# Mixture-of-experts stage on one Trainium2 core: rounding the expert weights to fp32r on ScalarE instead of GpSimd

## The reference

```
probs = softmax(xt @ Wg);  wts, idx = top_k(probs, 2);  wts = wts / sum(wts)
h1 = gelu(einsum('td,edf->etf', xt, W1) + b1[:, None, :])      # W1: 8 x 256 x 1024
ye = einsum('etf,efd->etd', h1, W2) + b2[:, None, :]           # W2: 8 x 1024 x 256
moe_out = sum(wts[..., None] * ye[idx, arange(T)[:, None], :], axis=1)
x = layernorm(x + (x_attn + moe_out))
```

## Time and profile before

| | |
|---|---|
| median of 3 runs | 4782.31 us (4779.12 to 4784.58) |
| the profiled execution | 4777.63 us, span 4775.8 us |
| busy in the whole span | PE 4253.5 us (89%), DVE 3625.5, ACT 3703.7, POOL 2061.1 |
| experts stage, from the first up to the last down | 4122.2 to 4675.5 us |
| mean granted TensorE clock | 0.942 |

### The profile page before, as it was taken

The page is one execution under the profiler, slowest core; times in us unless marked ns, Lnnn a source line. Parts: engine busy times, 40 slices in busy tenths (PEclk is TensorE's granted clock), DMA queues, the critical chain, the costliest instruction groups (busy, mean ns, idle before and its releaser), DMA issues. The chain is left out here.

```text
span 4775.8 us, 95820 instructions
## 1 busy us (share of the span) xinstructions
PE 4253.5 (89%) x22137; PEld 1697.9 (36%) x22137; DVE 3625.5 (76%) x7256; ACT 3703.7 (78%) x6958; POOL 2061.1 (43%) x1018
## 2 busy tenths in 40 slices
PE   7569999999999999999999999999999963499991
PEld 4322222222222222222222222222222243499991
DVE  3658898989899889988898998889898863133335
ACT  1347999999999999999999999999999841255551
POOL 0011343434344443434343443434343423788875
PEclk8777999999999999999999999999999985699995
DMA  2231010101001010101011010101010014334433
GB/s 78 101 83 17 0 17 0 17 0 17 5 12 17 0 17 0 17 0 17 0 17 16 2 17 0 17 0 17 0 17 0 0 51 140 123 138 137 137 115 114
DMA packets 105461, 176.13 MB, mean 37 GB/s; under 512 B 16512, under 2 KB 87552, under 8 KB 99072
## 3 DMA queue, kind: packets, MB, share of 16 engines
q1 hardware_dynamic: 86864, 146.17, 11.9%
q0 software_dynamic: 6336, 16.79, 1.1%
q10 hardware_dynamic: 12144, 12.06, 0.7%
HBM read 117.55 MB, written 57.15 MB: 37 GB/s over the span
## 5 line engine op out<-in xcount | busy, mean ns | idle before, releaser
L741 ACT ACTIVATE probs<-s_ps 128x512 f32<-128x512 f32 x4096 | 2430.6, 601 | 213.5 <-PE s_ps L683 161.3
L590 POOL TENSOR_TENSOR probs_low<-probs 128x1024 f16<-128x1024 f32 x640 | 1324.6, 2070 | 2082.9 <-ACT probs L741 2082.9
L804 DVE TENSOR_TENSOR probs_low<-probs 128x1024 f16<-128x1024 f32 x1408 | 1820.5, 1295 | 20.9 <-ACT probs L741 20.7
L797 DVE CUSTOM_DVE_ANT_0 excess<-b_ps,excess 128x512 f32<-128x512 f32 x2048 | 1401.9, 687 | 332.5 <-ACT excess L728 264.7
L683 PE MATMUL s_ps<-q_ring,k_ring 98*128 (+1 forms) x4096 | 1565.1, 384 | 13.8 <-ACT probs L741 8.6
L728 ACT ACTIVATE excess<-diff_ps 128x512 f32<-128x512 f32 x2048 | 1215.4, 594 | 57.9 <-PE diff_ps L627 48.9
L666 PE MATMUL o_ps<-probs,v_parts 128*64 128x512 bf16 x4106 | 854.1, 412 | 74.8 <-ACT o_here L733 72.2
L683 PEld LDWEIGHTS s_ps<-q_ring,k_ring 98*128 98x128 bf16 x4096 | 434.3, 106 | 1160.3 <-ACT probs L741 574.1
L627 PE MATMUL diff_ps<-kd_ring,q_ring 96*128 (+1 forms) x2048 | 801.1, 391 | 50.5 <-issue 38.2
L636 PE MATMUL b_ps<-k_ring,q_ring 96*128 (+1 forms) x2048 | 798.9, 390 | 11.5 <-DVE unit_max L797 10.7
L666 PE MATMUL o_ps<-probs_low,v_parts 128*64 128x512 f16 x4106 | 783.7, 378 | 0.0
(11 more groups left out here) (195 smaller groups left out, 3445.3 us busy)
## 6 DMA issues: line engine op xcount, KB each, us to landing
w_in<-in_W SPq DMA_DIRECT2D x46, 1024.0 KB, 4.9
q_ring<-qs_dram SPq DMA_DIRECT2D x96, 128.0 KB, 4.4
k_ring<-ks_dram SPq DMA_DIRECT2D x96, 128.0 KB, 7.1
slots_dram<-zero_rows SPq DMA_DIRECT2D x24, 512.0 KB, 6.4
rows_e<-slots_dram SPq DMA_DIRECT2D x24, 512.0 KB, 3.9
y_slots_dram<-y_out ACTq DMA_DIRECT2D x23, 512.0 KB, 4.1
qs_dram<-parts SPq DMA_DIRECT2D x16, 384.0 KB, 3.0
ks_dram<-parts SPq DMA_DIRECT2D x16, 384.0 KB, 4.2
```

The source lines that it names most:

```text
L590: nc.gpsimd.tensor_tensor(probs_low[:, t % BUFS, :, :], probs[:, t % BUFS, :, :], high[:, :, :, 1], ALU.subtract).then_inc(pool_low_done, 1)
L741: nc.scalar.activation(probs[:, t % BUFS, k, :], s2_ps[:, k, :], ACT.Exp).then_inc(exp_done, 1)
L797: nc.vector.tensor_tensor_reduce(excess[:, u % 2, :], b_ps[:, u % 2, :], excess[:, u % 2, :], 1.0, LEAST, ALU.add, ALU.max, unit_max[:, u ...
L804: nc.vector.tensor_tensor(probs_low[:, t % BUFS, :, :], probs[:, t % BUFS, :, :], high[:, :, :, 1], ALU.subtract).then_inc(low_done, 1)
```

## The change

The high parts of the weights are no longer made by GpSimd but by ScalarE, in four copies a tile of 128x1024 elements each. They stand inside ScalarE's tile j for the weights of tile j+1: the halves of `w1` after the `hidden_high` copies of steps 1 and 2, the halves of `w2` after those of steps 6 and 7. GpSimd keeps the subtractions, each behind a wait for its ScalarE copy; that of `w2` is now done in two halves (so there are four instructions, two for each matrix). `w_ready` counts four a tile, and TensorE waits for all four at the tile's start as before. So that the last tile rounds nothing, `per_tile` takes the last two tiles out of the loop.

```diff
-        W_OPS = 6
+        W_OPS = 4
...
-                body(0, 0, True)
-                with eng.Fori(0, (SLOT_TILES - 1) // 2) as it:
+                body(0, 0, True, False)
+                with eng.Fori(0, (SLOT_TILES - 3) // 2) as it:
                     for n in range(2):
-                        body(eng.snap(it * 2 + (n + 1)), (n + 1) % 2, False)
+                        body(eng.snap(it * 2 + (n + 1)), (n + 1) % 2, False, False)
+                body(SLOT_TILES - 2, 1, False, False)
+                body(SLOT_TILES - 1, 0, False, True)
...
-                pool.wait_ge(ups_done, j + 1)
-                pool.wait_ge(w1_full, j * 16)
                 w1 = w1_in[:, :, :].rearrange("p j (i t) -> p j t i", t=FT)
                 for half in range(HALVES):
-                    nc.gpsimd.tensor_tensor(w1_high[:, b, half, :, :], w1[:, half, :, :],
-                                            zero[:, :].unsqueeze(2).to_broadcast([P, FT, P]), ALU.add
-                                            ).then_inc(w_ready, 1)
-                pool.wait_ge(w_ready, j * W_OPS + 2)
-                for half in range(HALVES):
+                    pool.wait_ge(w1_rounded, j * HALVES + (half + 1 - HALVES))
+                    pool.sem_inc(pool_passed, 1)
                     nc.gpsimd.tensor_tensor(w1_low[:, b, half, :, :], w1[:, half, :, :],
                                             w1_high[:, b, half, :, :].bitcast(F32), ALU.subtract).then_inc(w_ready, 1)
+                pool.wait_ge(w_ready, j * W_OPS + 2)
+                pool.sem_inc(w1_split, 1)
+
+                for half in range(2):
+                    part = slice(FT // 2 * half, FT // 2 * half + FT // 2)
+                    pool.wait_ge(w2_rounded, j * 2 + (half - 1))
+                    pool.sem_inc(pool_passed, 1)
+                    nc.gpsimd.tensor_tensor(w2_low[:, b, part, :], w2_in[:, part, :], w2_high[:, b, part, :].bitcast(F32),
+                                            ALU.subtract).then_inc(w_ready, 1)
                 pool.wait_ge(w_ready, j * W_OPS + 4)
-                pool.sem_inc(w1_split, 1)
-
-                pool.wait_ge(hidden_used, j * FT + (4 - FT))
-                pool.wait_ge(w2_full, j * 16)
-                nc.gpsimd.tensor_tensor(w2_high[:, b, :, :], w2_in[:, :, :],
-                                        zero[:, :].unsqueeze(2).to_broadcast([P, FT, D]), ALU.add).then_inc(w_ready, 1)
...
                 pool.sem_inc(w2_split, 1)
...
-                pe.wait_ge(w_ready, j * W_OPS + 6)
+                pe.wait_ge(w_ready, j * W_OPS + 4)
...
+            def round_w1(j, b, half):
+
+                act.wait_ge(ups_done, j + 1)
+                act.wait_ge(w1_full, j * 16)
+                nc.scalar.activation(w1_high[:, b, half, :, :],
+                                     w1_in[:, half, :].rearrange("p (i t) -> p t i", t=FT), ACT.Copy).then_inc(w1_rounded, 1)
+
+            def round_w2(j, b, half):
+
+                act.wait_ge(hidden_used, j * FT + (4 - FT))
+                act.wait_ge(w2_full, j * 16)
+                part = slice(FT // 2 * half, FT // 2 * half + FT // 2)
+                nc.scalar.activation(w2_high[:, b, part, :], w2_in[:, part, :], ACT.Copy).then_inc(w2_rounded, 1)
...
                     nc.scalar.activation(hidden_high[:, f % 4, :], h_ps[:, f % 2, :], ACT.Copy).then_inc(high_done, 1)
+                    if f in (1, 2) and not last:
+                        round_w1(j + 1, 1 - b, f - 1)
+                    if f in (6, 7) and not last:
+                        round_w2(j + 1, 1 - b, f - 6)
                     if f == 4 and not first:
                         store(j - 1)
```

More of the change, by code:

```diff
@@ L1256, in experts @@
             sem("w1_full"), sem("w2_full"), sem("w1_split"), sem("w2_split"), sem("w_ready"))
+        w1_rounded, w2_rounded = sem("w1_rounded"), sem("w2_rounded")
         sync_passed, pool_passed = sem("sync_passed_e"), sem("pool_passed_e")
@@ L1292, in load_bias, with load @@
                 sp.dma_start(b2_here[:, b, :], dram["b2"][ds(e, 1), :].to_broadcast([P, D])).then_inc(bias_full[b], 16)
-            def load(j, b, first):
+            def load(j, b, first, last):
                 load_rows(j, b)
@@ L1323, in _, with split @@
             pool.wait_ge(zero_set, 1)
-            def split(j, b, first):
+            def split(j, b, first, last):
                 if first:
@@ L1330, in split @@
                     return
-                pool.wait_ge(ups_done, j + 1)
-                pool.wait_ge(w1_full, j * 16)
                 w1 = w1_in[:, :, :].rearrange("p j (i t) -> p j t i", t=FT)
                 for half in range(HALVES):
-                    nc.gpsimd.tensor_tensor(w1_high[:, b, half, :, :], w1[:, half, :, :],
-                                            zero[:, :].unsqueeze(2).to_broadcast([P, FT, P]), ALU.add
-                                            ).then_inc(w_ready, 1)
-                pool.wait_ge(w_ready, j * W_OPS + 2)
-                for half in range(HALVES):
+                    pool.wait_ge(w1_rounded, j * HALVES + (half + 1 - HALVES))
+                    pool.sem_inc(pool_passed, 1)
                     nc.gpsimd.tensor_tensor(w1_low[:, b, half, :, :], w1[:, half, :, :],
                                             w1_high[:, b, half, :, :].bitcast(F32), ALU.subtract).then_inc(w_ready, 1)
-                pool.wait_ge(w_ready, j * W_OPS + 4)
-                pool.sem_inc(w1_split, 1)
-                pool.wait_ge(hidden_used, j * FT + (4 - FT))
-                pool.wait_ge(w2_full, j * 16)
-                nc.gpsimd.tensor_tensor(w2_high[:, b, :, :], w2_in[:, :, :],
-                                        zero[:, :].unsqueeze(2).to_broadcast([P, FT, D]), ALU.add).then_inc(w_ready, 1)
[L1350 to L1353, removed]
+                pool.wait_ge(w_ready, j * W_OPS + 2)
[6 more added lines that the diff above has]
+                                            ALU.subtract).then_inc(w_ready, 1)
+                pool.wait_ge(w_ready, j * W_OPS + 4)
                 pool.sem_inc(w2_split, 1)
@@ L1392, in down, with tile @@
                 last.then_inc(hidden_used, 1)
-            def tile(j, b, first):
-                pe.wait_ge(w_ready, j * W_OPS + 6)
+            def tile(j, b, first, last):
+                pe.wait_ge(w_ready, j * W_OPS + 4)
                 pe.wait_ge(m_ready, j + 1)
```

## The result

The changed kernel takes 4925.12 us (median of 4 runs, 4924.56 to 4930.39) where the kernel before, measured beside it, takes 4783.1 us: 142 us more, ratio 1.0303 with a 95% interval of 1.0286 to 1.0319. The forecast was 4926 us, in a range of 4895 to 4950.

What follows compares the result with a forecast made beforehand. TensorE was taken to set the experts stage's pace. 22 tile starts x (4.5 us stall + 2.3 us clock) less 5.3 us for tile 2's incident gave +144 us, 4926 us on the median, range 4895 to 4950.

Steps and rivals of the forecast that it cites:

- TensorE sets the pace, GpSimd's relief buys nothing: Experts stage: TensorE is busy 24 of 24 us a tile and GpSimd is early, so removing GpSimd work gains nothing by itself.
- The incident of tile 2: At tile 2's start GpSimd's rounding slowed `m_low` and TensorE idled 2.71 us; without that rounding 5.3 us are gained, once.
- The stall: At each of 22 tile starts TensorE waits for the second w2 subtraction: 4.5 us a tile, bounds 3.9 to 5.0.
- The chain: Tile's end: ScalarE's step 7 and second w2 rounding, GpSimd's two w2 subtractions, the first held by `m_low`, then TensorE starts.
- The clock: Behind each stall TensorE's matmuls run slow at a lowered clock: 2.3 us a tile, ends 2.0 and 2.6; 0 if it holds.
- The w1 copies: Two copies mid-tile fit ScalarE's idle time in steps 1 to 3: 1.06 to 1.9 us each, at no cost.
- The cover of 2.5 us a copy: ScalarE's slack in mid-tile was said to hide the two w1 copies up to 2.5 us each.
- Loop and semaphores: Two tiles out of the loop and some more waits: taken as 0, between -1 and +5 us in all.
- The sum: 22 tile starts x (4.5 + 2.3) = 149.6, less 5.3: +144 us, making 4926 us, 3.0% slower.
- Rival 1: The stall comes but the clock stays up or falls at few tiles: +94, 4876 us; at half the tiles 4901; chance 0.12.
- Rival 2: Strided w1 copies slip out of ScalarE's gaps: at 3 us a copy 22 us more, 4948 us; chance 0.04.
- rival 3: Not slower: the second w2 half is finished before TensorE empties its queue, and tile 2's incident goes: 4777 us; chance 0.04.

Runs made afterwards that it cites:

- e1_late_wait: Changed kernel, TensorE waiting at a tile's start only for the w1 subtractions, for w2's before its first down: 4778.74 us, ratio 0.9995 to the kernel before.
- e2_w2_at_3_4: Changed kernel with the two w2 copies after steps 3 and 4 instead of 6 and 7: 4777.47 us, ratio 0.9992 to the kernel before.
- e3: Kernel before with only the last two tiles taken out of the loop: 4781.45 us, ratio 0.9998 to the kernel before.
- e5: Changed kernel with the w2 copies after steps 4 and 7 instead of 6 and 7: 4894.32 us, ratio 1.025 to the kernel before.
- e6: Changed kernel with the w2 copies after steps 4 and 6 instead of 6 and 7: 4845.11 us, ratio 1.0151 to the kernel before.
- e4: Changed kernel with 18 unused matmuls of 512 columns filling the stall at each tile's end: 4881.58 us, ratio 1.0206 to the kernel before.
- e7: e1_late_wait with the two w1 copies reading contiguously instead of with a stride of 8 elements: 4769.53 us, ratio 0.9992 to the kernel before.
- e8: e1_late_wait with each w1 copy issued twice: 4827.06 us, ratio 1.011 to the kernel before.

## Why the prediction was right

- **TensorE sets the pace, GpSimd's relief buys nothing.** Right: in e1_late_wait and e2_w2_at_3_4 GpSimd has 8 to 9 us a tile less to do (11.9 us in e1's row, 20.3 in the earlier trace rows) and the tile takes the same time.
- **The incident of tile 2.** Right in its cause (e3 has it, e1 does not). Its 5.3 us are the only gain in sight. In the medians e1 and e2 stand 3 and 4 us under before, too little to tell from no change; in the traces, from the first up to the end of the last down, the stage takes 553.5 us before and 553.2 in e3, 547.9 and 547.8 in e1 and e2, 5.6 us less.
- **The stall, 4.5 us forecast, 4.58 measured.** The chain went as written, with small errors that cancel in part. ScalarE was through with its second rounding 0.5 us earlier in the tile than forecast, which did not count, since GpSimd was still at the first half; GpSimd's second half ended 0.2 us earlier than forecast; and the last hand-over, to TensorE, took 0.4 us where 0.1 was taken. That the first half is held by `m_low` is shown by e5 and e6.
- **The clock, 2.3 us forecast, 2.32 measured.** e4 shows that it is the clock and that idleness is its cause. The size is in part luck: it is the middle of two bounds, 2.0 and 2.6, that came from one stretch each at tile 0 and tile 2 of the kernel before, and what it met is a mean over tiles that lose from 1.5 to 2.4 us. With gaps shorter by only 0.9 us the mean is 1.96 (e5). The Trainium skill ("TensorE: Matmul & The Clock Gate", Part 1) would leave the ramp out as under 1% of a span; here it is 22 x 2.32 = 51 us, 1.04% of 4925 and over a third of the loss. The section on HAM oscillation of the same page of the Trainium skill, where the transition is paid at every tile, is the one that fits, and the trace agrees: each of tiles 1 to 21 takes 29.9 us or more, where the stall alone would make 28.3.
- **The w1 copies.** Right that they cost nothing (e1, e7), wrong in their price: 2.34 us in the mean (2.24 to 2.48) is above the upper bound of 1.9, which took over VectorE's factor of 1.76 for the stride. ScalarE's is 2.2 (2.34 to 1.05). The two are not quite alike: VectorE's contiguous instruction was one of 2048 elements, halved, ScalarE's one of 1024. The Trainium skill ("SBUF — State Buffer", the note on cachelines) says that a crossing into a new line is paid, and the trace agrees so far as the strided copy costs more (2.34 us against 1.05); that the lines are the reason is not shown here. The cover of 2.5 us a copy was just enough by the prediction's sum; by e8 it is 3.1 / 2 + 1.54 = 3.1.
- **Loop and semaphores**: 0 forecast. The loop's form costs 0 by e3; the new waits cost TensorE nothing that shows, by the tiles of e1 and e2, which start 23.7 us apart as before.
- **The sum.** 22 x 6.90 - 5.3 = 146.5 by the tile distances, 147.8 between the two spans, 142 between the medians. In the traces the experts stage is 146.6 us longer (700.1 to 553.5), 2 more than the forecast 144; that the median came within 1 us of the forecast is luck, since the stages outside differ by 5 us and more from execution to execution (the experts stage begins 5 us earlier in the changed kernel's trace, and combine takes 6 us longer). Rival 1 (the clock stays, or falls at part of the tiles) is what happens at gaps of 2.3 us, in e6, and did not at 4.6. Rival 2 was priced with copies of 3 us, which took 2.34, and rival 3 needed a wait that is met in time; neither came.

No version is measurably faster than the kernel before: TensorE is busy for all of a tile in e1 and e2, so what is left to gain in this stage lies with its work.

## What to carry to other kernels

Moving work to an idle engine is not yet a gain or a loss: look where in the consumer's order it lands, and for which wait it is the last to arrive. A wait for all parts at the top of a tile is worth splitting into the part needed at once and the part needed later; moving one such wait took back all of the 142 us here, with the same work on the same engines. And a stall on TensorE is to be priced with the slow stretch behind it, which added half as much again.

## What was not expected of the hardware

- How much a gap costs in clock depends on its length, and with the same length on the moment. Gaps of 0.7 and 1.6 us cost 0 (e8); of 2.3 us 0 in some tiles and 1.5 in others, 1.2 in the mean (e6); of 2.7 us 2.7 (tile 2 of the kernel before, once); of 3.7 us 1.96 in the mean, and at tile 1 0 (e5: the first two rows are 27.44 apart, which is 23.73 and the gap); of 4.6 us 2.32 in the mean, 1.5 to 2.4. Matmuls of no use in the gap bring the cost to 0 (e4).
- ScalarE pays more than VectorE for reading fp32 from SBUF with a stride of 32 bytes: 2.2 times the contiguous copy (2.34 us to 1.05, e7) against 1.76.
- GpSimd's subtraction takes 2.33 to 2.40 us alone and 2.94 us when it starts 0.5 us into VectorE's `m_low` (e6).
